# u*B of three late turns by ScalarE with tokens on partitions, four by GpSimd, in a selective scan kernel

## The reference

```python
delta, Bmat, Cmat = split(einsum('bld,kd->blk', x, W_xproj))
delta = softplus(einsum('blr,dr->bld', delta, W_dt) + b_dt)
deltaA = exp(delta[..., None] * A)
BX = delta[..., None] * Bmat[:, :, None, :] * x[..., None]
h = dA * h + bx            # over the tokens
y = einsum('bdn,bn->bd', h, c) ;  y = y + D * x
# second layer, for each expert e
out = where(top1_idx == e, (x @ (w_scaled * mask_e).T) * top1_w, out)
```

## Time and profile before

| | us |
|---|---|
| median of 3 runs | 338.56 |
| lowest and highest run | 338.29, 340.86 |
| the profiled execution | 340.22 |
| its span, first to last instruction | 338.4 |

### The profile page before, as it was taken

One profiled execution on the slowest core, in us unless ns is written; L12 is line 12 of the kernel. 1 busy time (PEld: TensorE's weight loads), 2 busy tenths in 40 slices (PEclk: granted clock), 3 DMA queues, 4 the chain that ended last, 5 costly groups with the idle time before them and its releaser, 6 DMA issues.

```text
span 338.4 us, 3987 instructions
## 1 busy us (share of the span) xinstructions
PE 259.0 (77%) x1246; PEld 147.3 (44%) x1246; DVE 279.0 (82%) x350; ACT 166.3 (49%) x231; POOL 270.1 (80%) x157
## 2 busy tenths in 40 slices
PE   0882999999999989798999688899600387985670
PEld 0431354534345644355655344545500155864550
DVE  3979998999999999999999999999897633653360
ACT  1389964588786464565554543333645023323210
POOL 0586998899999999999999999999477614554562
PEclk9997699999999999799999999999955597999965
DMA  7419899999989789999999766610034489564100
GB/s 228 153 44 330 222 306 308 392 402 354 402 315 330 291 307 302 331 313 318 293 317 322 232 229 232 225 63 0 2 125 187 187 275 393 186 175 173 48 1 0
DMA packets 36963, 78.80 MB, mean 233 GB/s; under 512 B 5123, under 2 KB 16909, under 8 KB 36944
## 3 DMA queue, kind: packets, MB, share of 16 engines
q1 hardware_dynamic: 24496, 63.67, 56.0%
q10 hardware_dynamic: 9632, 8.57, 7.8%
q0 software_dynamic: 2816, 6.32, 5.0%
HBM read 63.55 MB, written 17.09 MB: 238 GB/s over the span
## 4 chain that ended last, share of the span: by engine, by line
PE 40%; DVE 18%; issue 16%; ACT 8%; POOL 7%; DMA 4%; another core or an unknown queue 3%; SPq 1%; ACTq 0%; DVEq 0%; POOLq 0%
PE bank L1191 18%; DVE bank L857 7%; DVE xs_sb L862 6%; PE bank L1368 5%; POOL sorted_tokens L501 5%; PE bank L1156 4%; PE bank L1109 2%; DMA xs_sb<-sorted_tokens 2%; PE bank L1103 2%; POOL out_dram L511 2%; PE bank L1130 2%; DMA x_sb<-in_L_attn_x_dram 2%; PE bank L1131 2%; PE bank L1182 1%
## 5 line engine op out<-in xcount | busy, mean ns | idle before, releaser
L445 POOL TENSOR_TENSOR xs_sb<-xs_sb,cb 128x1024 f32<-128x1024 f32 x63 | 147.4, 2371 | 3.8 <-DMA cb<-bc_rows 1.6
L1191 PE MATMUL bank<-xs_sb,cst 128*128 128x512 f32 x256 | 123.9, 608 | 2.0 <-ACT xn L638 1.6
L862 DVE TENSOR_TENSOR_SCAN xs_sb<-dA,bank 128x1024 f32<-128x1024 f32 x45 | 102.9, 2287 | 1.6
L1191 PEld LDWEIGHTS bank<-xs_sb,cst 128*128 128x128 f32 x256 | 48.0, 194 | 44.5 <-issue 34.5
L511 POOL DMA_INDIRECT out_dram<-cb,to_token x32 | 31.8, 994 | 31.9 <-DVE cb L1018 12.2
L857 DVE TENSOR_TENSOR bank<-bank,rows 128x1024 f32<-128x1024 f32 x44 | 53.3, 1211 | 1.2 <-PE bank L1156 1.0
L633 ACT ACTIVATE dA<-rows,a_neg 128x1024 f32<-128x1024 f32 x44 | 49.7, 1139 | 0.2
L438 POOL TENSOR_TENSOR xs_sb<-xs_sb,rows 128x1024 f32<-128x1024 f32 x19 | 45.6, 2399 | 0.3 <-POOL wT L457 0.3
L862 DVE TENSOR_TENSOR_SCAN xs_sb<-bank,xs_sb 128x1024 f32<-128x1024 f32 x19 | 43.2, 2275 | 1.4 <-ACT bank L633 1.0
L1368 PE MATMUL bank<-wT,xn 128*128 x240 | 33.4, 297 | 8.1 <-ACT xn L759 6.6
L618 ACT ACTIVATE wT<-bank 128x512 f16<-128x512 bf16 x32 | 19.0, 594 | 37.2 <-PE bank L1172 37.0
(11 more groups left out here) (158 smaller groups left out, 341.8 us busy)
## 6 DMA issues: line engine op xcount, KB each, us to landing
cb<-bc_rows SPq DMA_DIRECT2D x64, 512.0 KB, 5.9
xs_sb<-bc_rows SPq DMA_DIRECT2D x19, 512.0 KB, 6.8
sorted_tokens<-wT SPq DMA_DIRECT2D x32, 257.0 KB, 10.3
mask_sb<-_L_ffn_expert_masks_dram ACTq DMA_DIRECT2D x32, 256.0 KB, 6.7
xs_sb<-sorted_tokens SPq DMA_DIRECT2D x6, 1028.0 KB
xs_sb<-sorted_tokens SPq DMA_DIRECT2D x2, 514.0 KB
x_sb<-in_L_attn_x_dram SPq DMA_DIRECT2D x4, 256.0 KB, 4.5
x_sb<-in_L_attn_x_dram SPq DMA_DIRECT2D x2, 512.0 KB, 7.5
```

Of the source, the lines that this page charges most:

```text
L445: pool.tensor_tensor(here, here, cb[:, j, :], ALU.mult).then_inc(s_prod, 1)
L862: dve.tensor_tensor_scan(h[:, k % HELD, :], decays, bx, 0.0, ALU.mult, ALU.add).then_inc(s_scan, 1)
L1191: mm = pe.matmul(yacc[:, c * HC:(c + 1) * HC], ident, h[:, j, c * HC:(c + 1) * HC], start=first, stop=last, skip_group_check=True)
```

## The change

Of the last sixteen turns (48 to 63) GpSimd makes u*B for states 2, 5, 7, 10 (it was 2, 5, 8, 11, 14). For states 9, 12 and 15, that is turns 57, 60 and 63, u*B is made another way: u with tokens on the partitions (`u_T`) is scaled by ScalarE with one number per partition, B of that token (`b_T`), in eight pieces of 128 tokens, and TensorE transposes the eight pieces into the PSUM buffer from which the scan reads. VectorE then doesn't multiply in these turns. The other nine turns of the group are as before, which makes VectorE's multiplications 9 where they were 11.

For it B of batch 1 is transposed once: TensorE in iteration 19 (`turn_b`, eight transposes of 32x128, behind delta_sum), and ScalarE copies it in the same iteration (`b_T_out`, between delta_out and bc_move). u of the last group is transposed in two halves in iterations 52 and 53 (`turn_u`, `u_T_out`), each four transposes and one copy of 128x512. `u_T` lies where the last part of yT is written at the end, `u_b_T` in the mask buffers, and `b_T` is a new tile.

```diff
--- before.py
+++ after.py
@@ -22,6 +22,8 @@
 RING = 4
 HELD = 6
 POOL_STATES = (2, 5, 8, 11, 14)
+LATE_POOL_STATES = (2, 5, 7, 10)
+LATE_ACT_STATES = (9, 12, 15)
 FIRST_POOL_STATES = (2, 5, 8, 12)
 GROUPS = B * DH
 TURNS = GROUPS * N
@@ -96,6 +98,7 @@
         h_and_prod = xs_sb[:, :, :, :].rearrange("p s t c -> p (s t c)")
         h = h_and_prod[:, 0:HELD * L].rearrange("p (a l) -> p a l", a=HELD)
         b_apart = h_and_prod[:, HELD * L:(HELD + 2) * L].rearrange("p (a l) -> p a l", a=2)
+        b_T = sb("b_T", [P, LB, N])
         cb = sb("cb", [P, RING, L])
         route = cb[:, 2:4, :]
         mask_sb = sb("mask_sb", [P, 4, DH, D])
@@ -201,6 +204,11 @@
         s_c = [sem(f"c_loaded{j}") for j in range(RING)]
         s_bload = [sem(f"b_loaded{j}") for j in range(2)]
         s_bfed = sem("b_of_turn_fed_loaded")
+        s_btps = sem("b_transposed")
+        s_btsb = sem("b_transposed_evacuated")
+        s_utps = sem("u_transposed")
+        s_utsb = sem("u_transposed_evacuated")
+        s_abx = sem("transposed_bx_ready")
         s_gbx = sem("bx_ready_from_gpsimd")
         s_da = sem("decay_ready")
         s_bx = sem("bx_ready")
@@ -294,9 +302,17 @@
-        pool_turns = [k for k in range(TURNS) if k % N in (POOL_STATES if k >= N else FIRST_POOL_STATES)]
+
+
+        pool_turns = [k for k in range(TURNS) if k % N in (FIRST_POOL_STATES if k < N else POOL_STATES if k < TURNS - N else LATE_POOL_STATES)]
+        act_turns = [TURNS - N + n for n in LATE_ACT_STATES]
         of_pool = [sum(1 for p in pool_turns if p < k) for k in range(TURNS + 1)]
-        of_dve = [k - of_pool[k] for k in range(TURNS + 1)]
+        of_act = [sum(1 for p in act_turns if p < k) for k in range(TURNS + 1)]
+        of_psum = [k - of_pool[k] for k in range(TURNS + 1)]
+        of_dve = [of_psum[k] - of_act[k] for k in range(TURNS + 1)]
+        u_T = yT[:, 1, 1, :].rearrange("p (c d) -> p c d", c=LB)
+        u_b_T = mask_sb[:, 0:2, :, :].rearrange("p j h i -> p (j h i)").rearrange("p (c d) -> p c d", c=LB)
+        BT_AT, UT_AT = MASK_FROM - 1, {MASK_FROM + E: 0, MASK_FROM + E + 1: 1}
 
         def b_buffer(k):
             return b_apart[:, of_pool[k] % 2, :]
@@ -631,6 +647,27 @@
                     if k >= RING:
                         act.wait_ge(s_scan, k - 3)
                 act.activation(to, delta[:, dh, b * L:(b + 1) * L], ACT.Exp, scale=a_neg[:, dh, n:n + 1]).then_inc(s_da, 1)
+
+            def b_T_out():
+                act.wait_ge(s_btps, 1)
+                act.activation(b_T[:, :, :], w_ps[:, 0:LB * 2 * N].rearrange("p (c n) -> p c n", n=2 * N)[:, :, 0:N],
+                               ACT.Copy).then_inc(s_btsb, 1)
+
+            def u_T_out(c):
+                act.wait_ge(s_utps, c + 1)
+                act.activation(u_T[:, 4 * c:4 * c + 4, :].rearrange("p c d -> p (c d)"), w_ps, ACT.Copy).then_inc(s_utsb, 1)
+
+            def act_bx(k):
+                i, n = of_act[k], k % N
+                if i == 0:
+                    act.wait_ge(s_utsb, LH)
+                    act.wait_ge(s_btsb, 1)
+                    act.wait_ge(s_mps, E)
+                else:
+                    act.wait_ge(s_bready, of_psum[act_turns[i - 1]])
+                for c in range(LB):
+                    ins = act.activation(u_b_T[:, c, :], u_T[:, c, :], ACT.Copy, scale=b_T[:, c, n:n + 1])
+                ins.then_inc(s_abx, 1)
 
             def y_out(g, c=None):
                 act.wait_ge(s_sum, N * (g + 1) if c is None else TURNS + c)
@@ -661,8 +698,14 @@
                     decay(k + 1)
                 if AHEAD <= k + 2 < TURNS and k + 2 not in pool_turns:
                     decay(k + 2)
+                if k in UT_AT:
+                    u_T_out(UT_AT[k])
+                if k + 2 in act_turns:
+                    act_bx(k + 2)
                 if k in COPY_AT:
                     delta_out(COPY_AT[k])
+                if k == BT_AT:
+                    b_T_out()
                 if k == MASK_FROM - 12:
                     for e in range(4):
                         load_mask(e)
@@ -853,9 +896,10 @@
                         dve.wait_ge(s_bfed, 16)
                         dve.wait_ge(s_xnsb, DH * LH + DH)
                     else:
-                        dve.wait_ge(s_bready, of_dve[k] + (k < FED))
-                    dve.tensor_tensor(bx, rows_of_b, u[:, dh, b * L:(b + 1) * L], ALU.mult).then_inc(s_bx, 1)
-                    dve.wait_ge(s_bx, of_dve[k] + 1)
+                        dve.wait_ge(s_bready, of_psum[k] + (k < FED))
+                    if k not in act_turns:
+                        dve.tensor_tensor(bx, rows_of_b, u[:, dh, b * L:(b + 1) * L], ALU.mult).then_inc(s_bx, 1)
+                        dve.wait_ge(s_bx, of_dve[k] + 1)
                 dve.wait_ge(s_da, k + 1)
                 if k >= HELD:
                     dve.wait_ge(s_sum, k - HELD + 1)
@@ -1157,6 +1201,24 @@
                                    bc3[:, cols], start=True, stop=True)
                 mm.then_inc(s_bready, 1)
 
+            def turn_b():
+                for c in range(LB):
+                    mm = pe.transpose(w_ps[:, 2 * N * c:2 * N * c + 2 * N], xd[lanes, c * P:(c + 1) * P], ident[lanes, lanes])
+                mm.then_inc(s_btps, 1)
+
+            def turn_u(c):
+                for t in range(4):
+                    at = L + c * HC + t * P
+                    mm = pe.transpose(w_ps[:, t * P:(t + 1) * P], u[:, DH - 1, at:at + P], ident)
+                mm.then_inc(s_utps, 1)
+
+            def turn_bx(k):
+                pe.wait_ge(s_abx, of_act[k] + 1)
+                pe.wait_ge(s_scan, k - 1)
+                for c in range(LB):
+                    mm = pe.transpose(b_ps[k % 2][:, c * P:(c + 1) * P], u_b_T[:, c, :], ident)
+                mm.then_inc(s_bready, 1)
+
             def turn_signs(dst):
                 for ic in range(DH):
                     for oc in range(DH):
@@ -1226,7 +1288,9 @@
                     pe.wait_ge(s_bc3, 4 * LH)
                 if k == FED + 1:
                     pe.wait_ge(s_bc3, 2 * LH)
-                if FED < k + 1 < TURNS and k + 1 not in pool_turns:
+                if k + 1 in act_turns:
+                    turn_bx(k + 1)
+                elif FED < k + 1 < TURNS and k + 1 not in pool_turns:
                     b_rows(k + 1)
                 if k >= N and n == LAG:
                     pe.wait_ge(s_yT, g)
@@ -1241,6 +1305,18 @@
                 prepare(k)
                 if k in ADD_AT:
                     delta_sum(ADD_AT[k])
+                if k == BT_AT:
+                    pe.wait_ge(s_abs, B * DH * LH)
+                    turn_b()
+                if k in UT_AT:
+                    pe.wait_ge(s_wt, E)
+                    if UT_AT[k]:
+                        pe.wait_ge(s_utsb, 1)
+                    turn_u(UT_AT[k])
+                if k == MASK_FROM:
+                    pe.wait_ge(s_btsb, 1)
+                if k == min(HALF_LOGITS_AT):
+                    pe.wait_ge(s_utsb, LH)
                 if k == ROUTER_AT:
                     pe.wait_ge(s_dsb, B * DH * LH)
                     pe.wait_ge(s_u, B * DH * LH)
```

## The result

The changed kernel takes 340.94 us (median of 20 runs, 337.87 to 342.62); the kernel before, run 20 times beside it, takes 340.24 (338.29 to 342.73), so that the three runs shown ahead of the prediction lay low. The medians stand 0.70 us apart, the means 0.61 (340.83 and 340.22, standard error 0.40). The measured ratio of the changed kernel to before, which is formed over the rounds of a measurement, is 1.005, 95% interval 1.0028 to 1.0072: 1.0 to 2.4 us slower. The forecast was 0.6 us slower.

The account below looks back on a forecast made before the run. VectorE and GpSimd were taken as full, TensorE nearly, with VectorE's scans on the path. +2.14 (turn 21) - 2.48 (two multiplications) + 0.95 (turn 58) = +0.6 us, so 339.2 us on the median 338.56; range 336.9 to 341.0.

Parts of the forecast that it names:

- Behind the scans nothing is changed: After the last scan, second layer norm statistics to scatter: no added cost, x1_out ready as before within some tenths.
- stall before scan 21: Early part: ScalarE's b_T_out waits for TensorE's turn_b, delaying decay(21); VectorE stalls 2.6 us, 2.14 left at turn 48.
- late turns, 48 to 63: Last sixteen turns: two VectorE multiplications saved, 2.48 us, less a 0.95 us wait for GpSimd at turn 58.
- both waits: VectorE waits at turn 21 for ScalarE's decay and at turn 58 for GpSimd's u*B; 339.2 us, chance 0.50.
- eight transposes of 32 rows take about the 0.11 us each: TensorE's turn_b in iteration 19, behind delta_sum: sums begin at 97.65, so the transposes end near 98.65 us.
- ScalarE's activations and the clock: Turns 57, 60, 63: eight activations at 0.3 us each, 2.4 us; granted clock stays 1.00 by the rows.
- one wait only: Rival: the stall at turn 21 comes but turn 58's wait for GpSimd does not; 338.2 us, chance 0.17.
- faster: Rival: ScalarE's early wait is absorbed, transposes found done or the decay early; 337.0 to 336.1 us, chance 0.10.
- the cover that I gave TensorE: Turns 57 to 63: TensorE's added transposes stay hidden with 1.5 us of cover; without it each costs 0.5.
- the wait at scan 24: Early part: before's wait for decay(24), 0.40 us (0.48 by the starts), vanishes and offsets part of the turn 21 stall.
- clock rival: Rival: transposes lower TensorE's granted clock in turns 57 to 63; 341 to 342 or 345 us, chance 0.10.
- theory 1: From the experiments: the difference is that of the scans, made of early stall, turn 58's wait and saved multiplications.

Follow-up runs that it names:

- run 20: No label of a follow-up run: the kernel before was run 20 times beside the changed kernel; median 340.24 us (338.29 to 342.73).
- again_3: The changed kernel with no edit, measured a fourth time, beside the kernel before on a further chip; ratio 0.9998 (0.9970 to 1.0025).
- layout_only: The kernel before with only the new tile b_T and five semaphores declared, no instruction changed, against the kernel before; ratio 1.0004 (0.9979 to 1.0029).

## Why the prediction was wrong, and what of it was right

The forecast was +0.6 us, a difference too small to tell. The ratio tells one of +1.7 (1.0 to 2.4). The step of the prediction that failed is "Behind the scans nothing is changed", a term put at nothing: it measured +0.30 to +0.31 us in all four traces of the changed kernel. The stall before scan 21 was mis-sized besides, at 2.6 us where the first trace has 2.08 (2.14 and 1.72 at scan 48). These two errors pull in opposite directions, so that the first trace's sum of +0.57 meets the forecast of +0.6 in part by luck.

| term, us | forecast | first trace | other traces of the changed kernel |
|---|---|---|---|
| stall before scan 21, by its start | +2.6 | +2.08 | +2.41, +1.98, +0.62 |
| left of it at scan 48 | +2.14 | +1.72 | +1.67, +1.16, +0.02 |
| late turns, 48 to 63 | -1.53 | -1.46 | -1.36, -1.28, -1.45 |
| scan 63 to scatter | 0 | +0.31 | +0.31, +0.30, +0.31 |
| sum | +0.6 | +0.57 | +0.62, +0.18, -1.12 |

All are differences to the one trace of before that was there at the prediction. The three other traces with its instructions take 149.69, 150.01 and 151.14 us from scan 20 to the scatter, as against its 150.35, so a sum is good to some 0.8 us; the rows of the late turns and of the way to the scatter are firmer.

*The mechanism of both waits was right*, place and releaser: ScalarE's queue at iteration 19, and GpSimd's three products ahead of turn 58's u*B. (The profile does not name the decay as scan 21's releaser; that the stall is gone with the copy moved does.) The second's size was right too (0.95 forecast; 0.93, 0.79, 0.71 and 0.95 measured).

*The early stall.* The step "eight transposes of 32 rows take about the 0.11 us each" priced them by 128-row ones and put turn_b at 1.0 us; it took 0.68 to its end and 0.61 to the next matmul. That is 0.32 of the 0.5 us between 2.6 and 2.1; most of the rest is that TensorE came to turn_b 0.18 us sooner behind scan 20's start. And the stall isn't a constant: it is the lateness of decay(21) against a scan that has its own lateness, with an idle time from 0.54 in the execution with late C rows to 2.33 in another. By the prediction's own sign, that it is wrong if scan 21 waits under 2 us, two of the four traces (1.90 and 0.54) speak against it.

*Behind the scans.* The saved time arrives there less 0.31 us. The variance step waits for GpSimd's L498, and this for product 62, which waits for scan 62. In the changed kernel GpSimd is ahead enough to stand idle 0.78 us for scan 62, as against a queue of products before; the scatter gains what GpSimd gains (230.04 as against 230.55), and that is less than what the last scan gains (227.50 as against 228.34). I followed VectorE alone behind the scans. The row was there to be read: the same step took 1.02 us in before's timeline and ended with GpSimd's operation.

*ScalarE's activations and the clock* were as forecast: 2.43 us for eight (0.3 each; the forecast took 2.4), and a granted clock of 1.00 between 206 and 231 us with transposes in place of matmuls. The Trainium skill's rule on transposes (page TensorE: Matmul & The Clock Gate, section "Part 4: PE-mode transpose") made no difference here, as the rows had it.

*The rival "one wait only"* fell: the four traces of the changed kernel have a wait at turn 58 of 0.71 to 0.95 us. Of "faster", with the early wait absorbed, one of the four traces is a case (-1.12 us, again_3), though by late C rows and not by a decay that was early; no ratio shows it. And the cover that I gave TensorE (1.5 us) was counted with GpSimd's wait in place. With the wait away, TensorE was late twice.

*Two slips in the working.* The sum takes 0.46 us off for the wait at scan 24 where its own reading is 0.48. The clock rival's "one to two uncovered turns make 341 to 342" does not follow from its prices: at 1.15 us a turn they are 340.4 to 341.5, with 0.93 more for each turn's transposes 341.3 to 343.4. Neither touches the outcome.

*The number.* The forecast of 339.2 us was 0.6 above a median of 338.56 from three runs; over 20 runs before has 340.24. That is 1.7 us of sampling in the base, more than any error in a term. The range to 341.0 held 340.94 by luck.

*What stays open.* The stretches explain 0.57 us, on the first chip, and the medians (0.70) and means (0.61) of its runs ask for no more. If the ratio is right, at least 0.4 us more was lost there, and no run here shows where. The other three measurements, 1.0016, 1.0004 and 0.9998, are near the traces' sums or within their scatter; equal kernels give 1.0014 and 0.9986. layout_only shows no cost of layout and semaphores, on another chip; that the rest lies in the second layer, which took 11 us longer on the first chip, is only a guess. Neither theory is fully held up: theory 1 has the traces, and its sum is too small for that first interval.

## What to carry to other kernels

A small instruction that waits costs what is queued behind it: b_T_out is 0.28 us long and cost 2 us at the next scan, because it stood ahead of a decay that a scan needed; look for the place where its input is long done and its engine has idle time, and the price goes to nothing (12.40 us as against 13.97 from scan 20 to 24, in one trace each). Where three engines are nearly full, taking work from the fullest makes one wait appear behind another (GpSimd, then TensorE by way of ScalarE). Mending the early waits alone gave 1.0 us by the stretches, mending GpSimd's wait without ScalarE's order nothing in scans 48 to 63, and all three together 2.3. An engine's last step can hang on one that nobody followed, as the variance step did on GpSimd. Compare such kernels by stretches between two instructions that both have, and measure two equal kernels too, since whole times of one kernel strayed by nearly 5 us here (337.87 to 342.62). A ratio and the medians beside it can differ by more than the effect: look at both.

## What the runs showed of the hardware that I had not expected

- VectorE's step on 128x8 numbers took 0.68 to 1.89 us and ended within 0.1 us of GpSimd's running operation in all 13 traces that have it at its full length of 7.9 to 8.0 us; with this one cut to half it took 0.17. A tiny instruction of VectorE can so be as long as what GpSimd has left to do.
- An activation of 128x128 with a scale per partition, read from a tile, holds ScalarE for 0.29 us ((2.43 - 0.39) / 7) and is 0.386 us long; the plain copies of the earlier trace rows hold it for 0.19 and are 0.29 long.
- Eight fp32 transposes of 32x128 take 0.61 us of TensorE to the next matmul, eight of 128x128 take 0.93, both at a granted clock of 1.00.
- The time up to scan 20 differed by 5 us between executions with the same instructions there (94.21 to 99.25). In the longest VectorE waited 2.8 us for GpSimd there, behind 4.0 us of GpSimd's waits for C rows; in the shortest GpSimd waited 2.6 us for them and VectorE not at all for GpSimd.
